# Order of VectorE's waits at the end of a recurrence step

## What is computed

```python
def step(h, x_t):                       # h: 4 x 128
    proj = h @ W
    score = jnp.einsum('bsh,bh->bs', enc_hiddens, proj)      # 77 context rows
    attn = jax.nn.softmax(score, axis=-1)
    context = jnp.einsum('bs,bsh->bh', attn, enc_hiddens)
    inp = jnp.concatenate([x_t, context], axis=-1)
    gx = inp @ kernel + bias
    gh = h @ recurrent_kernel
    ...
    z = jax.nn.sigmoid(xz + hz)
    r = jax.nn.sigmoid(xr + hr)
    cand = jnp.tanh(xh + r * hh)
    h_new = z * h + (1.0 - z) * cand
    return (h_new, h_new)
```

## Time and profile before

| | us |
|---|---|
| median of 3 runs | 3105.05 |
| lowest, highest | 3101.61, 3105.86 |
| span of the profiled execution | 3108.8 |
| of it the recurrence's loop | 1983 |

### The profile page before, as it was taken

The page is one execution under the profiler, slowest core; times in us unless marked ns, Lnnn a source line. Parts: engine busy times, 40 slices in busy tenths (PEclk is TensorE's granted clock), DMA queues, the critical chain, the costliest instruction groups (busy, mean ns, idle before and its releaser), DMA issues. The chain is left out here.

```text
span 3108.8 us, 131004 instructions
## 1 busy us (share of the span) xinstructions
PE 2731.3 (88%) x54162; PEld 1800.4 (58%) x54163; DVE 2144.2 (69%) x8143; ACT 1712.7 (55%) x5762; POOL 995.6 (32%) x1992
## 2 busy tenths in 40 slices
PE   7999999887877999898999898999989877777768
PEld 4666666575455555565666565666656544444438
DVE  5666666773433888688888688777868766776653
ACT  4666666533443666576766576666657543333322
POOL 2000000230100666355666355555535311000015
PEclk9999999999878999999999999999999999999989
DMA  4000000000011000010000010000001000000013
GB/s 141 5 5 7 5 5 5 11 1 4 16 37 35 7 14 31 3 38 10 11 10 31 3 44 4 10 7 11 27 3 37 4 3 3 3 4 3 4 45 80
DMA packets 41078, 56.49 MB, mean 18 GB/s; under 512 B 6238, under 2 KB 27688, under 8 KB 40360
## 3 DMA queue, kind: packets, MB, share of 16 engines
q1 hardware_dynamic: 36392, 42.46, 4.3%
q0 software_dynamic: 4096, 5.67, 0.9%
HBM read 42.45 MB, written 5.67 MB: 15 GB/s over the span
## 5 line engine op out<-in xcount | busy, mean ns | idle before, releaser
L2183 POOL TENSOR_TENSOR gru_terms<-gru_states,gru_signs 128x8 f32<-128x8 f32 x512 | 104.2, 203 | 1180.9 <-DVE gru_states L2470 1077.7
L2103 ACT ACTIVATE gru_p<-gru_ps_sg,gru_negmax 128x78 f32<-128x78 f32 x512 | 167.5, 327 | 355.6 <-DVE gru_negmax L2439 350.4
L2107 ACT ACTIVATE gru_th_r<-gru_pre_r 128x32 f32<-128x32 f32 x512 | 118.8, 232 | 406.7 <-DVE gru_pre_r L2450 406.7
L1691 PE MATMUL gru_ps_sg<-ctx_gate_w,gru_p_t 128*4 128x64 f32 x12288 | 268.4, 221 | 0.1
L368 ACT ACTIVATE self_probs<-self_sc,self_negmax 128x512 f32<-128x512 f32 x256 | 174.4, 685 | 166.1 <-DVE self_negmax L425 166.1
L1936 PE MATMUL gru_ps_sg<-score_w,gru_states 128*4 128x78 f32 x4096 | 165.5, 234 | 94.3 <-DVE gru_states L2470 93.4
L2159 POOL TENSOR_SCALAR bg_probs<-bg_probs,bg_arsum 128x256 f32<-128x256 f32 (+2 forms) x192 | 241.0, 1255 | 19.0
L2443 DVE STREAM_TRANSPOSE gru_p_t<-gru_p 128x96 f32<-128x96 f32 x512 | 142.7, 279 | 112.1 <-ACT gru_p L2103 111.9
L2439 DVE TENSOR_REDUCE gru_negmax<-gru_ps_sg 128x1 f32<-128x78 f32 x512 | 121.7, 238 | 135.4 <-PE gru_ps_sg L1936 132.0
L1940 PE MATMUL gru_ps_own<-late,gru_states 128*4 128x128 f32 x4096 | 208.7, 276 | 0.0
L1691 PEld LDWEIGHTS gru_ps_sg<-ctx_gate_w,gru_p_t 128*4 128x4 f32 x12288 | 172.9, 86 | 38.4 <-issue 0.3
(11 more groups left out here) (421 smaller groups left out, 7391.5 us busy)
## 6 DMA issues: line engine op xcount, KB each, us to landing
bg_w<-in_moe_w SPq DMA_DIRECT2D x48, 256.0 KB, 2.9
bg_wa<-in_wqkv SPq DMA_DIRECT2D x24, 192.0 KB, 2.3
moe_w<-in_moe_w SPq DMA_DIRECT2D x16, 256.0 KB, 2.9
best_w_sb<-in_ec_w SPq DMA_DIRECT2D x16, 256.0 KB
cross_scratch<-ctab_raw SPq DMA_DIRECT2D x16, 154.0 KB
cross_outs<-cross_scratch POOLq DMA_DIRECT2D x4, 576.0 KB, 6.1
late<-in_late SPq DMA_DIRECT2D x1, 2269.5 KB
self_w_sb<-in_wqkv SPq DMA_DIRECT2D x8, 192.0 KB, 2.4
```

Source lines behind the costliest of these rows:

```text
L1691: last = pe.matmul(bank[32 * c:32 * c + B, 0:hi - lo], p_t[:, 32 * k:32 * k + B], gate_w[:, k, 96 * c + lo:96 * c + hi], start=k == 0, sto ...
L2103: act.activation(p[:, 0:CTX + 1], ps_s[:, 0:CTX + 1], ACT.Exp, bias=negmax[:, 0:1], accum_out=total[:, 0:1])\
```

## The change

In VectorE's code the two waits for GpSimd (`s_olds`, `s_hist`) move from the state scan to the turn of z, behind `s_thz`. At the state scan, `s_tc` is now written first and `s_onez` second. No instruction that computes is added, removed or moved.

```diff
                 dve.wait_ge(s_thz, t + 1)
+                dve.wait_ge(s_olds, t + 1)
+                if t:
+                    dve.wait_ge(s_hist, t)
                 dve.transpose(th_z_t[:], th_z[:]).then_inc(s_tz, 1)
                 dve.wait_ge(s_cand, t + 1)
                 dve.transpose(terms[:, 0:96:3], cand[:]).then_inc(s_tc, 1)
+                dve.wait_ge(s_tc, t + 1)
                 dve.wait_ge(s_onez, t + 1)
-                dve.wait_ge(s_olds, t + 1)
-                if t:
-                    dve.wait_ge(s_hist, t)
-                dve.wait_ge(s_tc, t + 1)
                 at = (t + 1) % 2 * 3 * B
                 dve.tensor_tensor_scan(states[:, at:at + 3 * B], factors[:], terms[:, 0:3 * B], 0.0, ALU.mult, ALU.add)\
                    .then_inc(s_h, 1)
```

## The result

| | before | after |
|---|---|---|
| median, runs of the result | 3105.45 | 3081.06 |
| lowest, highest | 3101.61, 3110.28 | 3080.27, 3084.98 |
| span of the profiled execution | 3108.8 | 3082.8 |
| first to last state scan | 1982.8 | 1958.6 |

The ratio of the times is 0.993, with an interval of 0.9913 to 0.9946, so 17 to 27 us. The forecast was 3082 in a range of 3073 to 3092. The profiled execution took 3084.98 us.

What follows compares the result with a forecast made beforehand. The prediction took a loop through four engines, not TensorE, as the bound; 325 steps x 0.07 us = 22.75 us off the 3108.8 us span gave 3086.0, or 3082 from the runs' median of 3105.05; range 3073 to 3092.

Steps and rivals of the forecast that it cites:

- The bound: Whole step: a loop through four engines, 3.87 us a step, bounds the kernel, not TensorE's 88% busy share.
- the 325: Steps whose scores start 0.055 to 0.056 us after the state scan; each was to become 0.07 us shorter.
- the 186: Steps whose scores start later, nearly all 0.12 us and more after the scan; an earlier state was to give nothing.
- TensorE's spare time doesn't run out: TensorE before the scores: 0.28 us of idle, four times the gain, was to leave enough room in the 325 steps.
- Part one: State scan: a wait that it carries itself, here the turned candidate's, takes 0.03 us behind its signal.
- Part two: Factors' wait in a wait instruction ahead of the scan: scan 0.105 us after the factors instead of 0.175, 0.07 us earlier.
- the 0.12 and 0.14 us: L2271 after L2018's end, with one wait and with two; taken to show one wait fewer saves 0.02 to 0.03 us.
- Part three: GpSimd's waits ahead of the turn of z: no price, handled beside L2459 under a cover of 0.29 us.
- The sum: Whole loop: 325 steps x 0.07 us = 22.75 us gained, by bounds 15.3 and 30.9 us.
- the engine emptying itself: Rival at the state scan: the 0.13 us gap stays whatever carries the wait; no change, 3105 us; chance 0.09.
- half of the gain would be eaten further on: Rival: background work holds scores or exponentials in half of the 325 steps; 11 us gained, 3094 us; chance 0.09.
- a pair ahead of z is handled only after L2459: Rival at the turn of z: factors 0.11 us later, scan 0.04 later, 13 us slower, 3118 us; chance 0.05.

Runs made afterwards that it cites:

- e2: Changed kernel with the old order at the scan (factors' wait first), GpSimd's waits still moved ahead of the turn of z; ratio 0.9984 to the kernel before.
- e4: Kernel before, nothing moved away from the scan, only the turned candidate's wait written second instead of last; ratio 0.9955 to the kernel before.
- e5: Changed kernel with the old terms' wait back at the scan, so the factors' wait is first of a pair; ratio 0.9945 to the kernel before.
- e1: Kernel before with the turned candidate's wait written first at the scan, GpSimd's waits left there; ratio 0.9930 to the kernel before.
- e3: Changed kernel with the factors raising the turned candidate's semaphore, so the scan carries one wait and none stands ahead; ratio 0.9917 to the kernel before.
- b0: The kernel before once more, unedited, as a single run; loop from first to last state scan 1981.3 us.
- e0: The changed kernel again, no edit, on the chip of the first experiments; ratio 0.9928 to the kernel before.
- e6: Changed kernel with more long-passed waits ahead of the turn of z, five pairs in all; ratio 1.0178 to the kernel before.
- e8: The one-semaphore kernel of e3 again, no further edit, on another chip; ratio 0.9892 to the kernel before.
- e9: One-semaphore kernel with TensorE's mask matmul behind the first background piece instead of the last; ratio 0.9951 to the kernel before, 16 us slower than e8.

## Why the prediction was right, and where it was not

**The bound.** The loop through four engines, and not TensorE's 88%, decided. In the median the two kinds of step behaved as forecast: 0.073 us for the 325, nothing for the 186, whose scores moved from 0.136 to 0.211 us behind the scan. The dose follows too: 0.03, 0.043, 0.045, 0.075, 0.088 and 0.098 us a step (e2, e4, e5, the change, e1, e3) shortened the loop by 12, 16, 17, 23 to 28, 26 and 28 to 33 us against b0. One step of the working failed, though. That TensorE's spare time doesn't run out was read from a single step with 0.28 us of idle. It did run out in the 31 steps that left the 325 (29 of these left in e0 too), and the prediction had named such a turn as a sign of being wrong. In 26 of them the scores now start 0.133 to 0.135 us after the mask matmul, as in the 186. Before, that distance was 0.20 us in most of these, so only 0.07 us were to spare. In e3, with a still earlier state, 56 left.

**Part one** (a wait that the scan carries takes 0.03 us behind its signal) was right: 0.034 in e3, where nothing else is late.

**Part two** had the right size for a partly wrong reason. The scan starts 0.101 us after the factors, where 0.105 was worked out; the gain of a step is 0.075 for 0.07, and what is late next is the path of z, by 0.02 us over that of the candidate. But the working took 0.025 us off a pair for having one wait less. That is right for a pair whose first wait comes last (0.132, and 0.103 for a single one in e2). The number of waits was only half of it: a pair costs 0.132 if its first wait comes last and 0.087 if its second does, with 0.101 for a single one in between. Had the old kernel's pair been the other way round, the same subtraction would have given a wrong sum.

Of the two rows that the 0.12 and 0.14 us came from the earlier trace rows, neither measures what it was taken for. L2271's wait instruction starts 0.036 to 0.038 us after the start of the state scan ahead of it, and so do the other wait instructions behind a state scan in this kernel (0.037 in the median of 323 steps): it was VectorE's own queue that it came behind, not L2018's signal. The difference of the two rows still is the right one, since the two wait instructions last 0.021 and 0.050 us. L1429's 0.11 us stands: its wait instruction starts 0.036 us after the exponentials' end.

**Part three** was right: no price, and the turn of z 0.03 us after its tanh. The one pair needs 0.11 of the 0.31 us from the start of L2459 to that of the turn; e6 shows that five pairs are more than the cover holds.

**The sum** was 22.75 us. The loop shrank by 24.2, and the medians differ by 24.4. That 325 x 0.075 is 24.4 as well is partly luck: the 294 steps that stayed gave 22.8 us, the 31 that left took back 3.0, and the 186, which were to give nothing, gave 4.4, where the two profiles of the kernel before differ by 2.6 in them.

**The rivals.** That the 0.13 us were the engine emptying itself, and with it the rule quoted from the Trainium skill ("VectorE: DVE Perf Modes", "The DRAIN you can't avoid", that a semaphore between operations costs nothing extra), is refuted for waits that stand in instructions of their own: 0.132, 0.103, 0.089 and 0.034 us between the same two VectorE operations, by the place of the waits alone. The prediction added that the trace agrees with the rule for a carried wait, and that holds only for one whose signal has long come. In the step of the earlier trace rows:

```profile
2700.93 0.25 DVE L2450 SCALAR_TENSOR_TENSOR gru_pre_r<-gru_ps_sg,gru_rtotal,gru_own 128x32 f32<-128x32 f32 x1
2701.10 0.24 DVE L2452 SCALAR_TENSOR_TENSOR gru_own<-gru_ps_sg,gru_rtotal,gru_own 128x32 f32<-128x32 f32 x1
2701.26 0.24 DVE L2455 SCALAR_TENSOR_TENSOR gru_pre_z<-gru_ps_tz,gru_rtotal,gru_own 128x32 f32<-128x32 f32 x1
```

L2452 has no wait and starts 0.08 us before the end of L2450; L2455 carries one for TensorE and starts 0.08 us before the end of L2452. A carried wait for the very instruction ahead starts its own 0.03 us behind that one's end (L1427, and the scan in e3).

That half of the gain would be eaten further on didn't happen, though the 31 steps are a small case of it. That a pair ahead of z is handled only after L2459 didn't happen either: its record starts 0.014 us after the start of L2459. A late turn of z does reach the state scan, as e6 shows, but there by a row of five pairs that is longer than its cover.

Two differences are explained in part. The runs of e2 gave 5 us while its loop has 12: the profiled execution of e2 was 3.0 us under the median of its runs and that of b0 2.2 us above the kernel before's, and at the same clock the runs give 7. The loops of e3 and e8 differ by 5 us at equal distances: e3's profiled execution was the fastest of its six (3061.93 us, clock 0.979), e8's the slowest of its four (3078.60 us, 0.971). What stays open is what holds the remaining 101 of the 186 steps, and why the weight load behind the moved mask matmul starts late in e9.

## What to carry to other kernels

Of the waits ahead of an instruction on the path that closes a loop, let the instruction carry the one that comes last; if another is nearly as late, put it on the same semaphore (here the quickest, e3), or as the second wait of a pair whose first has long passed. Try the order first: here it gave the whole gain without any move (e1). Waits that have long passed can be moved under an instruction that runs anyway, as long as they fit there. Look at the distance between an end and the next start in a timeline: on VectorE 0.03 us was a carried wait here, 0.09 to 0.13 us a wait instruction. And count in all steps, not in one, how many have the spare time that a gain needs.

## What the runs showed of the hardware

- On VectorE, ahead of the state scan, a wait instruction starts 0.036 to 0.038 us after the end of the instruction that signals, takes 0.021 us with one wait and 0.050 with two, and the next instruction starts 0.044 us after it. With the first of two waits passed and the second open, it ends 0.044 to 0.045 us after the end of the instruction that signals the second (e1, e4).
- Wait instructions are not handled before the instruction ahead has started: the first stands 0.014 us behind the start of L2459 in e6, and in the kernel before the history's wait 0.014 us behind the start of L2463. In a row, pairs stand 0.097 us apart (e6). Behind a state scan that has a wait instruction ahead of it, the next wait instruction starts 0.037 us after the scan's start (median of 323 steps, before and changed kernel), and 0.014 us where the scan has none (e8).
- Where nothing is waited for, a VectorE instruction starts before the one ahead has ended: L2452 0.083 us before the end of L2450, in the median of the kernel before's 512 steps.
- A 78-column bf16 matmul between a group of 512-column and a group of 128-column fp32 matmuls cost TensorE 0.2 us more there than at the end of the row, directly ahead of the scores (e9 against e8, median of 87 steps). The first weight load of the group behind it then started with its matmul instead of 0.43 us ahead.
